# Attention with products in bursts: six bursts of two or three steps in place of eight of two, and 128 rows in scores and maxima

## The reference

```
h = layernorm(x)
q = h @ Wq.T + bq + ocr_bias;  k = h @ Wk.T + bk;  v = h @ Wv.T + bv      (split into 16 heads of 32)
scores = q k^T / sqrt(32) + 0.1 * (|i - j| <= 2)
x = x + softmax(scores) @ v @ Wo.T + bo
x = x + quantised(layernorm(x)) @ quantised(weight).T + bias
```

## Time and profile before

| | |
|---|---|
| time, median of 3 runs (lowest to highest) | 4166.92 us (4161.44 to 4179.65) |
| the profiled execution: its time, its span | 4178.3 us, 4176.5 us |
| granted TensorE clock, mean | 0.989 |
| busy: TensorE, VectorE, ACT, GpSimd | 97%, 80%, 58%, 73% of the span |
| attention stage, about | 620 to 3720 us |
| chain that ended last, by engine | PE 77%, DVE 14%, ACT 4%, DMA 4% |

### The profile page before, as it was taken

The page is one execution under the profiler, slowest core; times in us unless marked ns, Lnnn a source line. Parts: engine busy times, 40 slices in busy tenths (PEclk is TensorE's granted clock), DMA queues, the critical chain, the costliest instruction groups (busy, mean ns, idle before and its releaser), DMA issues.

```text
span 4176.5 us, 59567 instructions
## 1 busy us (share of the span) xinstructions
PE 4036.3 (97%) x21328; PEld 2538.5 (61%) x21328; DVE 3359.0 (80%) x5630; ACT 2408.2 (58%) x4651; POOL 3034.4 (73%) x1118
## 2 busy tenths in 40 slices
PE   8999999999999999999999999999999999977998
PEld 6788875555555555555555555555555555536787
DVE  6444568888888888898888888888888888846886
ACT  2222216766667666766676677676676767652332
POOL 2111008888989888988888888988888888964552
PEclk9999999999999999999999999999999999988999
DMA  7888859999999999999999999998999899876664
GB/s 245 266 261 264 235 151 183 187 205 195 196 198 194 204 187 208 188 206 186 209 192 195 197 196 200 196 203 181 207 184 209 180 214 191 199 169 169 180 172 101
DMA packets 292270, 825.16 MB, mean 198 GB/s; under 512 B 28832, under 2 KB 95392, under 8 KB 229536
## 3 DMA queue, kind: packets, MB, share of 16 engines
q0 software_dynamic: 72960, 486.57, 59.2%
q1 hardware_dynamic: 219040, 335.09, 28.6%
HBM read 211.82 MB, written 156.24 MB: 88 GB/s over the span
## 4 chain that ended last, share of the span: by engine, by line
PE 77%; DVE 14%; ACT 4%; DMA 4%; issue 1%; SPq 0%; POOL 0%; POOLq 0%; ACTq 0%; DVEq 0%
PE ps_a L862 20%; PE ps_a L848 20%; PE ps_b L827 17%; PE ps_p L481 12%; DVE part_max L1039 8%; PE ps_b L893 3%; ACT p_sb L1015 3%; DVE p_sb L1066 2%; PE ps_b L940 2%; PE ps_b L873 1%; DMA o_first<-o_d 1%; DMA q_st<-shift 1%; PE ps_a L923 1%; DMA q_lo_d<-s_lo 0%; PE ps_t L499 0%
## 5 line engine op out<-in xcount | busy, mean ns | idle before, releaser
L1039 DVE TENSOR_REDUCE part_max<-ps_b 128x1 f32<-128x512 f32 x4016 | 2465.1, 678 | 379.4 <-PE ps_b L827 379.1
L1205 POOL TENSOR_TENSOR pair<-p_sb 128x2048 f32<-128x2048 f32 x512 | 2454.9, 4815 | 78.0 <-ACT p_sb L1015 59.3
L1015 ACT ACTIVATE p_sb<-ps_a 128x512 f32<-128x512 f32 x4096 | 2084.1, 614 | 726.0 <-PE ps_a L848 721.8
L862 PE MATMUL ps_a<-p_sb,v_sb 128*32 128x512 f32 x8192 | 993.5, 602 | 38.7 <-DVE p_sb L1066 23.0
L848 PE MATMUL ps_a<-q_st,k_odd 97*128 97x512 f32 x2048 | 845.2, 415 | 18.2 <-ACT p_sb L1015 17.8
L848 PE MATMUL ps_a<-q_st,k_even 97*128 97x512 f32 x2048 | 845.6, 413 | 7.5 <-PEq L163 3.8
L827 PE MATMUL ps_b<-k_odd,q_st 96*128 96x512 f32 x2048 | 813.6, 397 | 0.0
L827 PE MATMUL ps_b<-k_even,q_st 96*128 96x512 f32 x1968 | 783.4, 398 | 0.0
L848 PEld LDWEIGHTS ps_a<-q_st,k_odd 97*128 97x128 f32 x2048 | 388.0, 190 | 344.6 <-issue 214.6
L848 PEld LDWEIGHTS ps_a<-q_st,k_even 97*128 97x128 f32 x2048 | 388.2, 190 | 324.1 <-issue 218.5
L862 PEld LDWEIGHTS ps_a<-p_sb,v_sb 128*32 128x32 f32 x8192 | 224.1, 109 | 522.6 <-ACT p_sb L1015 321.5
(11 more groups left out here) (111 smaller groups left out, 2859.6 us busy)
## 6 DMA issues: line engine op xcount, KB each, us to landing
pair<-pair POOLq DMA_DIRECT2D x448, 1024.0 KB, 8.9
q_st<-q_hi_d SPq DMA_DIRECT2D x128, 256.0 KB, 7.2
xin<-in_x SPq DMA_DIRECT2D x16, 1024.0 KB, 8.7
xb_d<-xb SPq DMA_DIRECT2D x16, 1024.0 KB, 5.9
q_hi_d<-s_hi SPq DMA_DIRECT2D x64, 256.0 KB, 6.3
q_lo_d<-s_lo SPq DMA_DIRECT2D x64, 256.0 KB, 7.3
k_hi_d<-s_hi SPq DMA_DIRECT2D x64, 256.0 KB, 3.6
k_lo_d<-s_lo SPq DMA_DIRECT2D x64, 256.0 KB, 4.4
```

The costliest lines, as they stand in the source:

```text
L862: last = nc.tensor.matmul(ps_a[h * HD:(h + 1) * HD, RING_S, :], v_sb[:, kt, h * HD:(h + 1) * HD], p_sb[:, s % SLOTS, h, :], start=(kt == 0 ...
L1015: nc.scalar.activation(p_sb[:, s % SLOTS, h, :], ps_s[:, (HG * s + h) % RING_S, :], ACT.Exp, scale=SCALE).then_inc(p_ready, 1)
L1039: nc.vector.tensor_reduce(part_max[:, unit % 2, col, n:n + 1], ps_m[:, max_place(unit, j) % RING_M, :], AX.X, ALU.max).then_inc(max_taken, 1)
L1205: nc.gpsimd.tensor_tensor(pair[:, m % PAIR_RING], p_sb[:, s % SLOTS], p_sb[:, (s + 1) % SLOTS], ALU.add).then_inc(paired, 1)
```

## The change

- `weigh` is called in bursts of 2, 3, 3, 2, 3, 3 steps (`AT_ONCE`), each ending with step s - 3 (`BEHIND`). A unit's bursts stand at its steps 4, 7, 10, 12, 15 and at step 2 of the next unit, ahead of head 2. The last burst follows the loop.
- `add_keys` moves from step 11 to step 10, and with it ACT's copy of the sums and SP's store. ACT's copy of `ps_o` moves from step 1 to 2, SP's store of it from step 4 to 5.
- Scores and maxima read all 128 rows of `q_st` and of the keys. Rows 97 to 127 are set to zero once; row 96 of `q_st` must be zero while the unit's maxima are made, so behind each later load of q SP copies the zero row 97 onto it, as a fourth transfer that the unit's first maximum waits for.
- The rows of `k_even` and `q_st` are cleared by two memsets more in the projection stage (the maxima wait for them). For `k_odd` one memset of row 96 over 8192 columns at the start of attention gives way to four pairs of memsets of 2048 columns (32 rows to zero, one row to one), placed in GpSimd's list behind pairs 3, 5, 9 and 13.

```diff
@@ project: gpsimd
             pool.wait_ge(xb_ready, 5)
+            nc.gpsimd.memset(f32(q_st[ROWS:P]), 0.0).then_inc(ones_set, 1)
+            nc.gpsimd.memset(f32(k_even[ROWS:P]), 0.0).then_inc(ones_set, 1)
+            pool.wait_ge(ones_set, 2)
             nc.gpsimd.memset(f32(k_even[ROWS:ROWS + 1]), 1.0).then_inc(ones_set, 1)
-            pool.wait_ge(ones_set, 1)
+            pool.wait_ge(ones_set, 3)
@@ project: tensor, maxima ahead
+                    if place == 0:
+                        pe.wait_ge(ones_set, 3)
...
-                    nc.tensor.matmul(ps_t[:, place % RING_M, :], q_st[0:ROWS, unit, h, t * P:(t + 1) * P],
-                                     k_even[0:ROWS, n_, h, :], start=True, stop=True).then_inc(max_scored, 1)
+                    nc.tensor.matmul(ps_t[:, place % RING_M, :], q_st[:, unit, h, t * P:(t + 1) * P],
+                                     k_even[:, n_, h, :], start=True, stop=True).then_inc(max_scored, 1)
@@ attend_and_finish
-    SUM_AT = 11
+    SUM_AT = 10
+    AT_ONCE = (2, 3, 3, 2, 3, 3)
+    BEHIND = 3
...
+    ends = list(itertools.accumulate(AT_ONCE))
+
+    def at_once(s):
+
+        end = (s - BEHIND) % KT + 1
+        return range(s - BEHIND + 1 - AT_ONCE[ends.index(end)], s - BEHIND + 1) if s >= BEHIND and end in ends else ()
@@ sync
+                if unit >= RING_Q:
+                    sp.dma_start(f32(q_st[ROWS:ROWS + 1, i]), f32(q_st[ROWS + 1:ROWS + 2, i])).then_inc(q_loaded[i], 16)
...
-                        if kt == 4:
+                        if kt == 5:
                             store_o(unit - 1)
@@ tensor
-                    pe.wait_ge(q_loaded[unit % RING_Q], 48 * (unit // RING_Q + 1))
+                    pe.wait_ge(q_loaded[unit % RING_Q], 48 + 64 * (unit // RING_Q))
...
+                    if g == 1:
+                        pe.wait_ge(ones_set, 3 + 2 * (n + 1))
...
-                nc.tensor.matmul(ps_m[:, bank, :], q_st[0:ROWS, unit % RING_Q, h, t * P:(t + 1) * P],
-                                 k_st[g % 2][0:ROWS, n, h, :], start=True, stop=True).then_inc(max_scored, 1)
+                nc.tensor.matmul(ps_m[:, bank, :], q_st[:, unit % RING_Q, h, t * P:(t + 1) * P],
+                                 k_st[g % 2][:, n, h, :], start=True, stop=True).then_inc(max_scored, 1)
...
-                if h == 0 and s == KT * QC:
-                    pe.wait_ge(ones_set, 2)
...
-                                 k_st[unit // QC % 2][0:ROWS + 1, kt // TT, h, kt % TT * P:(kt % TT + 1) * P],
-                                 q_st[0:ROWS + 1, unit % RING_Q, h, :], start=True, stop=True).then_inc(scored, 1)
+                                 k_st[unit // QC % 2][:, kt // TT, h, kt % TT * P:(kt % TT + 1) * P],
+                                 q_st[:, unit % RING_Q, h, :], start=True, stop=True).then_inc(scored, 1)
...
             def burst(s):
-                if 3 <= s < ST + 3:
-                    weigh(s - 3)
-                    weigh(s - 2)
+                for x in at_once(s):
+                    weigh(x)
...
-            for s in range(ST + 2):
+            for s in range(ST + 1):
                 for h in range(HG):
-                    if s % 2 == 1 and h == HG // 2:
+                    if h == HG // 2:
                         burst(s)
...
+            for x in at_once(ST - 1 + BEHIND):
+                weigh(x)
@@ scalar
-                        if kt == 1:
+                        if kt == 2:
                             copy_o(unit - 1)
@@ gpsimd
-            nc.gpsimd.memset(f32(k_odd[ROWS:ROWS + 1]), 1.0).then_inc(ones_set, 1)
-            pool.wait_ge(ones_set, 2)
+
+            def odd_rows(n):
+
+                nc.gpsimd.memset(f32(k_odd[ROWS:P, n]), 0.0).then_inc(ones_set, 1)
+                pool.wait_ge(ones_set, 3 + 2 * n + 1)
+                nc.gpsimd.memset(f32(k_odd[ROWS:ROWS + 1, n]), 1.0).then_inc(ones_set, 1)
+                pool.wait_ge(ones_set, 3 + 2 * n + 2)
...
+                if m in (3, 5, 9, 13):
+                    pool.wait_ge(paired, m + 1)
+                    odd_rows((3, 5, 9, 13).index(m))
```

## The result

| | before | after |
|---|---|---|
| time, median (lowest to highest) | 4170.38 us (4161.44 to 4179.65) | 4215.64 us (4214.55 to 4222.42) |
| profiled execution: time, span | 4178.3, 4176.5 us | 4215.37, 4213.4 us |
| granted TensorE clock, mean | 0.989 | 0.991 |

Four runs of each; the ratio of after to before is 1.0118, interval 1.0102 to 1.0134. The change makes the kernel slower by 1.2%, 45 us by the medians and 37 by the two profiled executions, of which the one of before is among its kernel's slower runs. From the first score to the last it is 3121.9 us before and 3158.8 after: all of the 37 lies in the attention stage. Forecast were 4222 us and 1.3%.

What follows compares the result with a forecast made beforehand. TensorE was taken to set the attention stage's pace, VectorE and GpSimd close behind. Terms -41 - 33 + 122 + 7 = +55 us took the profiled 4178.3 to 4233, hence 4222 us for the median; range 4140 to 4265.

Steps and rivals of the forecast that it cites:

- Twelve maxima, four banks (+122): Attention stretches between bursts: TensorE's maxima wait for banks VectorE empties more slowly, costing 122 us, between 63 and 155.
- Two bursts fewer (-41): Attention units: two fewer entries into the 32-column products and back, 0.32 us each over 64 units, gain 41 us.
- waits that go (-33): Products a step later: waits for band factors go, half those for bank and shift; gain 33 us, between 22 and 68.
- Rows (nothing): Scores and maxima: widening to 128 rows costs and gains nothing per matmul.
- memsets (+7): GpSimd, first two units: eight k_odd memsets between pair sums cost 7 us, between 0 and 14.
- The join (nothing): Sums of keys: the joined transfer meets them a step earlier; nothing counted, upper bound 20 us for the slowest landings.
- The sum: Whole kernel: -41 - 33 + 122 + 7 = +55 us, slower by 1.3% in the median.
- The signs: Attention trace: burst lengths, maximum loads 0.60 apart, more bank waits, near-zero band-factor waits, unit about 49.2 us.
- (a): Maxima wait less and saved switches win, GpSimd stopping the gain at 46 us; 4115 to 4146 us, chance 0.17.
- (b): Cost and savings cancel, with bank waits costing 50 to 90 us: 4146 to 4188 us, chance 0.13.
- (d): Joined transfer late most of the time because GpSimd falls behind: 1 us a unit more, 4284 us, chance 0.05.
- (e): Widening to 128 rows has a price or prize no row shows, for instance a lower clock; chance 0.03.

Runs made afterwards that it cites:

- experiment 1: Kernel before with the change's bursts, SUM_AT and later copies and stores, but 96 and 97 rows and the old memset: 4211.61 us, ratio 1.0109.
- experiment 4: Changed kernel with eight bursts of two steps in place of six of two or three: 4174.54 us, 1.0019 against the kernel before.
- experiment 5: Changed kernel with VectorE's attention reduces reading 256 of the 512 columns of each bank: 4151.51 us, 0.9954 against the kernel before.
- experiment 3: Kernel before with products a step later, still eight bursts of two, on 96 and 97 rows: 4173.35 us, ratio 1.0014.
- experiment 2: Changed kernel with the schedule of before, keeping 128 rows, the memsets and the fourth transfer: 4176.53 us, 1.0020 against the kernel before.
- experiment 9: VectorE's reduces and GpSimd's pair sums both halved, in both kernels: changed kernel 4083.91 us (0.9804), kernel before 4154.9 us (0.9971).
- experiment 8: GpSimd's pair sums over half the columns, in three kernels: before 4209.84 us, changed with eight bursts of two 4234.42 us, changed 4215.0 us.
- experiment 7: Changed kernel with VectorE's band factors since the last burst moved to just ahead of each burst: 4384.5 us, 1.0522 against the kernel before.

## Why the prediction was right, step by step

**Twelve maxima, four banks (+122).** Right in mechanism and place, and the term that decides; shown by experiment 1 (the loss comes with the schedule), 4 (with the burst's length) and 5 (two thirds of it go when VectorE's reduces are lightened). Its size came out at 149, within 63 to 155. By place in the four units: a plain stretch of 24 takes 6.13 against 5.79, 0.34 late where 0.30 was worked out. With band factors in mid-stretch 7.35 (7 to 10 of the second unit) and 7.36 (15 to 2 behind the fourth), 1.22 and 1.23 more than a plain one where 1.23 was said. Behind a stretch of eight with factors 6.38 and 6.71, where 6.32 is usual for the second of these places: +0.25 and +0.39 for 0.31. What was left out: in the stretch 12 to 15 VectorE also copies the turned maxima (0.27 us), which makes it 6.32 and not 6.13; 0.2 x 62 = 12 us. With 4 x 62 x 0.04 = 10 this makes up most of the 27 that were missing. The 149 are counted against a stretch of 128-row matmuls that nothing holds (5.80). The ring's pace is the same on 96 and 97 rows (a plain stretch takes 6.13 in experiment 1 too), where a free stretch would be some 24 x 0.003 = 0.07 us longer; against that the ring costs about 131.

**Two bursts fewer (-41) and waits that go (-33).** Together 107 and not 74, or 117 with the waits inside bursts. The bursts themselves take 1.85, 2.71 and 3.57 exactly as the rows of before give them, 15.66 us a unit before and 15.40 after: 16 us. The rest of the 107 is in the stretches: (8 x 4.06 - 2 x 3.91 - 4 x 5.80) x 62 = 90 us. The recorded 41 has 25 of it, the cheaper way in and back, and 65 are left, with the waits inside bursts 75. Not all of this is waits: some 24 are the cheaper pairs of 128 rows (a clean stretch of 16 takes 3.95 in experiment 1 and 3.91 in the changed kernel). That leaves about 50 for waits, where 33 was taken and 68 was the upper bound. The reason given for half was that bank and shift waits overlap with slack; the mean of a stretch of 16, 4.06 before against a lowest of 3.89, had said that there was more to gain. But experiments 3 and 4 correct what this gain is: moving the products a step later gains nothing by itself (+0.1 and +0.2%), since the waits for VectorE's factors come back as waits for banks and for the joined transfer. In the changed kernel the two stretches of eight maxima in a unit are clean (3.91); what the other four were spared is hidden under the ring's waits.

The drain that TensorE: Matmul & The Clock Gate of the Trainium skill (Part 2, step 4) gives would have made this saving 14 us by the recorded estimate; no run isolates a change of tiling.

**Rows (nothing) and memsets (+7).** 8 us in experiment 2, 1 us between experiments 3 and 4, 4 us between experiment 1 and the changed kernel. The sum of the two terms fits these roughly; that the 7 is the memsets' is not shown. The 14.4 us (8 x 1.80) that they take on GpSimd are. "Nothing per matmul" was wrong: the pairs are 0.006 us shorter, up to 24 us in 62 units. The prediction read one gap in the last unit, 0.33 for 0.32, and not the pitch of many.

**The join (nothing).** Right in the changed kernel: 1.8 us of waits for it, a landing of 9.0 in the median. Where the ring does not hold TensorE up, waits near the bound of 20 come: 12.3 and 12.4 us in experiments 3 and 4, and 27.3 in experiment 5.

**The sum.** +55 was the sum, +42 is the ledger (+32 with the waits inside bursts), +45 the medians. Cost and savings were each too small, by 27 and by 33 (43), and the errors cancel. The mechanism and the sign were read from the rows; that the number came so close is in part luck.

**The signs.** Bursts of 1.85, 2.71 and six a unit; loads of maxima 0.60 apart at the end of a stretch; bank waits 14.7 to 254.3; no waits for band factors; steps 7 to 10 of the second unit over 1 us longer: all as written. The unit is 48.90 by the joins, where 49.2 was said.

**The rivals.** (a) said that GpSimd would stop a gain at about 46 us if the ring cost nothing. In experiment 5 two thirds of the ring's cost are gone, and the changed kernel is 18.5 us faster than before, with GpSimd's waits for exponentials down to 30.0. GpSimd does hold the gain down, and below 46. But it does so in part through the pair sums that VectorE's factors run into, which the rival did not have. Experiment 9 has the gain without both. (b) and (d) did not come. (e), a price or a prize of 128 rows, has 0.006 us a pair on the side of the prize and 8 us in all on that of the price.

**What stays open.** How much GpSimd by itself holds the kernel before: its load can't be changed without moving the merges against the shift transfer (experiment 8). What costs experiment 2 its 8 us. What a good place of the band factors in the stretches of twelve would give in all: experiment 7 freed the middle of the stretches, but put three factors in a row and ran into GpSimd, and no other place was tried.

## What to carry to other kernels

Before lengthening the stretch between two pauses of a producer, write down the pace at both ends of every ring that it feeds: here 0.47 us made, 0.60 taken, four banks, so eight go through without a wait and the twelfth is 0.43 late. Two switches saved at 0.32 us each are lost by four stretches at 0.34 each, before any interruption of the consumer is counted. A slower consumer that never shows as the bound (VectorE 80% busy) still sets how long the bursts of the producer may be.

Place what a consumer does between its items (band factors, a copy) where the ring has slack behind it, and check which other engine is at work on the same memory then. A consumer that becomes faster can come to such work too early: in experiment 5 half reduces made VectorE's factors last 499 us in place of 192. And where a queue of large transfers shares time with a small one that the bound engine needs, less work ahead of the large ones can make the kernel slower.

## What the runs showed of the hardware

- A VectorE multiplication of two operands in SBUF that begins during a GpSimd sum ends some 0.57 us behind it: 2.04 us in the mean against 0.68 for the others (experiment 5), three in 5.78 us (experiment 7).
- A shift transfer from SP landed about when the 1 MB merge in flight did: after 3.5 us in the median when issued 4.7 us behind it, after 5.6 when issued 3.3 us behind it. TensorE's matmuls waited 50.7 us for it in place of 4.0, and the kernel was 43 us slower with less work in it.
- Pairs of matmuls over 128 rows followed each other in 0.464 us in the median (experiment 2), over 96 and 97 rows in 0.470, at the same granted clock of 1.00.
